# Two heads on each half of the PE rows, score products in pairs, sums inverted before they are spread, and keys rounded by GpSimd

## The reference

```python
qh = split(q @ Wq.T + bq)          # 16 heads of 8
kh = split(k @ Wk.T + bk)
vh = split(v @ Wv.T + bv)
scores = jnp.einsum('bhqd,bhkd->bhqk', qh, kh) / jnp.sqrt(jnp.float32(D_K))
scores = jnp.where(mask[:, None, None, :] == 0, jnp.float32(-1000000000.0), scores)
attn = jax.nn.softmax(scores, axis=-1)
out = jnp.einsum('bhqk,bhkd->bhqd', attn, vh)   # then @ Wo.T + bo
```

## Time and profile before

| | |
|---|---|
| median of 3 runs | 3891.91 us (3890.11 to 3892.72) |
| profiled execution | 3887.87 us |
| its span, first to last instruction | 3886.1 us |
| busy: PE, PEld, DVE, ACT, POOL | 86%, 63%, 65%, 53%, 30% of the span |
| mean granted TensorE clock | 0.935 |
| stage L1a, loop over batches | about 428 to 1235 us |
| stage L2a, loop over batches | about 1546 to 2336 us |

### The profile page before, as it was taken

One profiled execution on the slowest core, in us unless ns is written; L12 is line 12 of the kernel. 1 busy time (PEld: TensorE's weight loads), 2 busy tenths in 40 slices (PEclk: granted clock), 3 DMA queues, 4 the chain that ended last, 5 costly groups with the idle time before them and its releaser, 6 DMA issues. The chain is left out here.

```text
span 3886.1 us, 96641 instructions
## 1 busy us (share of the span) xinstructions
PE 3344.9 (86%) x40650; PEld 2451.9 (63%) x40650; DVE 2514.8 (65%) x3568; ACT 2066.9 (53%) x3842; POOL 1154.1 (30%) x1125
## 2 busy tenths in 40 slices
PE   6776799999998575999999996579999999999988
PEld 4455577777776563777777774346666666666654
DVE  5633577677774224777777773667878878778751
ACT  3211366566664111666566663367677776776733
POOL 0012312222121214222222111135455455554520
PEclk9877899999999686999999997689999999999989
DMA  7932666555561314555554530100000000000000
GB/s 226 254 120 72 176 165 167 157 150 157 162 167 31 106 38 116 129 132 133 124 124 123 129 92 7 22 24 17 25 25 17 24 18 23 25 17 25 17 1 26
DMA packets 137255, 345.88 MB, mean 89 GB/s; under 512 B 56179, under 2 KB 79547, under 8 KB 136827
## 3 DMA queue, kind: packets, MB, share of 16 engines
q1 hardware_dynamic: 134139, 334.22, 32.3%
q0 software_dynamic: 2688, 5.51, 0.5%
HBM read 174.63 MB, written 17.09 MB: 49 GB/s over the span
## 5 line engine op out<-in xcount | busy, mean ns | idle before, releaser
L2040 POOL TENSOR_TENSOR l_S<-l_S,l_shift 125x448 f32<-125x448 f32 (+1 forms) x416 | 461.1, 1147 | 329.0 <-ACT l_shift L2272 326.5
L1338 ACT ACTIVATE L1a_probs<-ps 125x448 f32<-125x448 f32 x768 | 383.2, 544 | 202.8 <-PE ps L1238 189.5
L1338 ACT ACTIVATE L2a_probs<-ps 125x448 f32<-125x448 f32 x768 | 382.9, 544 | 203.3 <-PE ps L1238 189.9
L1371 DVE TENSOR_REDUCE L2a_chunk_max<-ps 112x1 f32<-112x1000 f32 x256 | 300.9, 1196 | 147.4 <-PE ps L1197 147.0
L1371 DVE TENSOR_REDUCE L1a_chunk_max<-ps 112x1 f32<-112x1000 f32 x256 | 300.9, 1196 | 135.9 <-PE ps L1197 135.4
L2150 PE MATMUL ps<-l_S,l_z 125*128 125x448 f32 x768 | 344.3, 545 | 0.0
L2253 ACT ACTIVATE ctx_stats<-ps 125x512 f32<-125x512 f32 (+1 forms) x416 | 248.3, 597 | 180.0 <-PE ps L2098 170.8
L2317 DVE TENSOR_REDUCE l_norms<-ctx_stats 125x8 f32<-125x512 f32 (+1 forms) x416 | 268.1, 675 | 77.9 <-ACT ctx_stats L2253 77.8
L2343 DVE SCALAR_TENSOR_TENSOR l_S<-ps,l_neg_cols,l_inv_norms 125x448 f32<-125x448 f32 x384 | 256.1, 679 | 81.8 <-PE ps L2119 77.1
L1197 PE MATMUL ps<-L1a_keys,L1a_queries 98*112 98x500 f32 x768 | 264.6, 427 | 47.0 <-DVE L1a_chunk_max L1371 20.5
L1197 PE MATMUL ps<-L2a_keys,L2a_queries 96*112 96x500 f32 x768 | 264.6, 427 | 45.8 <-DVE L2a_chunk_max L1371 20.5
(11 more groups left out here) (478 smaller groups left out, 7071.3 us busy)
## 6 DMA issues: line engine op xcount, KB each, us to landing
L1a_keys<-L1a_k_hi SPq DMA_DIRECT2D x256, 187.5 KB
L2a_keys<-L2a_k_hi SPq DMA_DIRECT2D x256, 187.5 KB
a_ctx_T<-in_ctx_T SPq DMA_DIRECT2D x32, 750.0 KB, 11.7
L1a_ctx_T<-in_ctx_T SPq DMA_DIRECT2D x32, 750.0 KB, 6.1
xn<-L_valid SPq DMA_DIRECT2D x32, 750.0 KB, 7.6
L1a_keys<-L1a_k_lo SPq DMA_DIRECT2D x128, 187.5 KB
L2a_ctx_T<-in_ctx_T SPq DMA_DIRECT2D x32, 750.0 KB, 6.4
L2a_keys<-L2a_k_lo SPq DMA_DIRECT2D x128, 187.5 KB
```

The costliest lines, as they stand in the source:

```text
L1338: nc.scalar.activation(probs[t % NPR][:, h * HQ // 2:(h + 1) * HQ // 2], s.ps[0:KP, i % 3, 0:HQ // 2], ACT.Exp).then_inc(probs_made, 1)
L1371: ins = nc.vector.tensor_reduce(chunk_max[:, n, 0:1], product, AX.XY, ALU.max)
L2040: nc.gpsimd.tensor_tensor(S[b % 2][0:r, t, :], S[b % 2][0:r, t, :], shift[0:r, :], ALU.add)\
```

## The change

The array's rows are used as two halves of 64. A group g now has two heads (u = 0) on rows 0 to 63 and two (u = 1) on rows 64 to 127: 3 x 16 rows of parts, mask and maxima in each half, 50 or 52 rows. Products are made in pairs, one on each half, into different PSUM banks. For a tile the scores are eight products of 112 columns in place of four of 224; both halves are asked for at the start of a step, and the exponentials of the two halves follow. The 12 rows items are two products of 500 columns each, as before, of 48 to 50 rows. The key pieces have 16 rows: 24 DMAs a batch for 12. The maxima take 4 DMAs for 2, the query terms 6 for 3, the mask rows 2 for 1. All 128 rows of the keys are set to one at the start. `k_hi` is made by GpSimd in front of each subtraction. The sums are transposed to 112 x 8, inverted, widened to 32 columns each by VectorE ("sums"), and spread by two products two steps later ("spread"); the norm multiplies from PSUM.

```diff
-    G, HPG = 4, 4
-    GR, GC4 = HPG * DK, HPG * SQ
+    G = 4
+    HALF = D // 2
+    GR = 2 * DK
     KQ = 3 * GR
...
+    ROWS = G * NKC
+    PIECES = 2 * G * 3
...
     step_items[5].append(("sums", -1, 0))
+    step_items[7].append(("spread", -1, 0))
...
+                def move(u, g, k, part):
+                    first, row = (2 * g + u) * GR, u * HALF + k * GR
+                    sp.dma_start(keys[b % NKB][row:row + GR, g, :].bitcast(F32), part[first:first + GR, :].bitcast(F32))\
+                        .then_inc(keys_moved, 16)
...
                 sp.wait_ge(k_hi_made, b * 2 + 2)
                 for g in range(G):
-                    for k in (0, 2):
-                        sp.dma_start(keys[b % NKB][k * GR:(k + 1) * GR, g, :].bitcast(F32),
-                                     k_hi[g * GR:(g + 1) * GR, :].bitcast(F32)).then_inc(keys_moved, 16)
+                    for u in range(2):
+                        for k in (0, 2):
+                            move(u, g, k, k_hi)
                 sp.wait_ge(k_lo_made, b * 2 + 2)
                 for g in range(G):
-                    sp.dma_start(keys[b % NKB][GR:2 * GR, g, :].bitcast(F32),
-                                 k_lo[g * GR:(g + 1) * GR, :].bitcast(F32)).then_inc(keys_moved, 16)
+                    for u in range(2):
+                        move(u, g, 1, k_lo)
...
                 for k, part in enumerate((max_hi, max_lo)):
-                    sp.dma_start(queries[b % NQ][SHIFT + k:SHIFT + k + 1, :, :].bitcast(F32), part[:, b % 2, :].bitcast(F32))\
-                        .then_inc(row_moved, 16)
+                    for u in range(2):
+                        row = u * HALF + SHIFT + k
+                        sp.dma_start(queries[b % NQ][row:row + 1, :, :].bitcast(F32),
+                                     part[u * G:(u + 1) * G, b % 2, :].bitcast(F32)).then_inc(row_moved, 16)
...
-            def take_keys_lo(b, n):
+            def split_keys(b, n):
                 cols = key_cols(n)
+                pool.wait_ge(scratch_dve, by_dve[("keys", b, n)])
+                if b and n == 0:
+                    pool.wait_ge(keys_moved, b * 16 * PIECES)
+                nc.gpsimd.tensor_copy(k_hi[:, cols], k_full[:, cols]).then_inc(k_hi_made, 1)
                 pool.wait_ge(k_hi_made, b * 2 + n + 1)
...
-                for half, (r, k) in enumerate(halves_of_row(n)):
-                    mm = nc.tensor.matmul(s.ps[0:RW, bank(item) + half, 0:KC],
-                                          queries[b % NQ][0:SHIFT, r // 2, r % 2 * RW:(r % 2 + 1) * RW],
-                                          keys[b % NKB][0:SHIFT, r // 2, k * KC:(k + 1) * KC], start=True, stop=True)
+                g, k = n // NKC, n % NKC
+                for u in range(2):
+                    mm = nc.tensor.matmul(s.ps[0:RW, bank(item) + u, 0:KC], queries[b % NQ][half(u, SHIFT), g, :],
+                                          keys[b % NKB][half(u, SHIFT), g, k * KC:(k + 1) * KC], start=True, stop=True)
...
+            def scores(b, t):
+
+                i = (b * KT + t) * 2
+                if t == 0:
+                    pe.wait_ge(row_moved, b * 64 + 64)
                 if i < 3:
                     pe.wait_ge(q_made, NCH)
-                else:
-                    pe.wait_ge(probs_made, i - 2)
...
+                if i >= 2:
+                    pe.wait_ge(probs_made, i - 1)
+                for g in range(G):
+                    for u in range(2):
+                        mm = nc.tensor.matmul(s.ps[0:KP, (i + u) % 3, g * RW:(g + 1) * RW],
+                                              keys[b % NKB][half(u, KS), g, t * KP:(t + 1) * KP],
+                                              queries[b % NQ][half(u, KS), g, :],
+                                              start=True, stop=True, skip_group_check=True)
+                        if g == G - 1:
+                            mm.then_inc(scores_made, 1)
...
-                nc.scalar.activation(k_hi[:, cols], k_full[:, cols], ACT.Copy).then_inc(k_hi_made, 1)
...
+            def invert_sums(item):
+                kind, b, n = item
+                dve.wait_ge(products, made[item])
+                nc.vector.reciprocal(inv[:, :, :].rearrange("p w j -> p (w j)"), s.ps[0:RW, bank(item), 0:8])\
+                    .then_inc(inverted, 1)
```

More of the change, by code:

```diff
@@ L887, in attention_16_heads, with half @@
     NQ, NKB, NPR, GT = 3, 3, 6, 3
-    PAIRS, SINGLES = RT, RT // 2
-    ROWS = PAIRS + SINGLES
-    PIECES = 12
+    ROWS = G * NKC
+    PIECES = 2 * G * 3
+    def half(u, n):
+        return slice(u * HALF, u * HALF + n)
     before_scores = [("rows", 1, 0), ("rows", 1, 1)]
@@ L1206, in turn, with turn_sums, spread_inverses @@
                 nc.tensor.transpose(s.ps[0:RT, bank(item), 0:RW], max_col[:, :], s.ident[0:RW, 0:RW]).then_inc(products, 1)
-            def spread_sums(item):
+            def turn_sums(item):
                 kind, b, n = item
                 wait_for_banks(pe, item)
-                if b == 0:
-                    pe.wait_ge(prep, 3)
                 pe.wait_ge(acc_taken, b + 1)
-                nc.tensor.matmul(s.ps[:, bank(item), 0:4 * SQ], sum_rows[:, :, :].rearrange("p j i -> p (j i)"),
-                                 acc[:, :], start=True, stop=True).then_inc(products, 1)
+                for w in range(2):
+                    mm = nc.tensor.matmul(s.ps[0:RW, bank(item), w * 4:(w + 1) * 4], acc[:, w * RW:(w + 1) * RW],
+                                          s.ident[:, DK:D:32], start=True, stop=True, skip_group_check=True)
+                mm.then_inc(products, 1)
+            def spread_inverses(item):
+                kind, b, n = item
+                wait_for_banks(pe, item)
+                pe.wait_ge(scratch_dve, by_dve[("sums", b, 0)])
+                for w in range(2):
+                    mm = nc.tensor.matmul(s.ps[:, bank(item), w * RW:(w + 1) * RW], inv_wide[:, w, :, :].rearrange("p j i -> p (j i)"),
+                                          s.ident[0:RW, 0:RW], start=True, stop=True, skip_group_check=True)
+                mm.then_inc(products, 1)
             def make(item):
@@ L1225, in make @@
                     turn(item)
[L1226 to L1232 removed]
+                elif item[0] == "sums":
+                    turn_sums(item)
+                else:
+                    spread_inverses(item)
+            def scores(b, t):
+                i = (b * KT + t) * 2
+                if t == 0:
+                    pe.wait_ge(row_moved, b * 64 + 64)
                 if i < 3:
                     pe.wait_ge(q_made, NCH)
[L1235 to L1241 removed]
+                if i >= 2:
+                    pe.wait_ge(probs_made, i - 1)
+                for g in range(G):
+                    for u in range(2):
+                        mm = nc.tensor.matmul(s.ps[0:KP, (i + u) % 3, g * RW:(g + 1) * RW],
[4 more added lines that the diff above has]
+                            mm.then_inc(scores_made, 1)
             def values(b, t):
@@ L1253, in values @@
                     j, c = h % 4, h // 4
+                    at = (h // 2 % 2 * 2 * G + h // 4 * 2 + h % 2) * SQ
                     mm = nc.tensor.matmul(s.ps[32 * j:32 * j + DK + 1, 3, c * SQ:(c + 1) * SQ], v[b % 2][:, t, h, :],
-                                          probs[t % NPR][:, h * SQ:(h + 1) * SQ], start=(t == 0 and c == 0),
+                                          probs[t % NPR][:, at:at + SQ], start=(t == 0 and c == 0),
                                           stop=(t == KT - 1), skip_group_check=True)
@@ L1308, in take @@
             def take(item):
-                if item[0] == "keys":
-                    take_keys(item)
-                elif item[0] == "values":
+                if item[0] == "values":
                     take_values(item)
@@ L1369, in empty_rows @@
                 product = s.ps[0:RW, bank(item):bank(item) + 2, 0:KC]
[L1370 to L1375 removed]
+                nc.vector.tensor_reduce(chunk_max[:, :, n // NKC, n % NKC], product, AX.X, ALU.max).then_inc(scratch_dve, 1)
                 if n == ROWS - 1:
@@ L1436, in _ @@
             dve.wait_ge(cut, 2)
-            nc.vector.tensor_reduce(group_mask[:, :], head_mask[:, :].rearrange("p (g h) -> p h g", h=HPG), AX.X,
-                                    ALU.add).then_inc(prep, 1)
-            nc.vector.tensor_copy(sum_rows[:, :, :], bcast(s.ident[:, DK:D:32], 32, 2)).then_inc(prep, 1)
+            nc.vector.memset(group_mask[:, :], 1.0).then_inc(prep, 1)
+            dve.wait_ge(prep, 2)
+            for u in range(2):
+                nc.vector.tensor_reduce(group_mask[half(u, KQ), :],
+                                        head_mask[half(u, KQ), :].rearrange("p (m e) -> p e m", e=2), AX.X,
+                                        ALU.add).then_inc(prep, 1)
             for item in prologue:
```

137 lines of the change are left out of this document (63 added, 74 removed).

## The result

The changed kernel takes 4500.9 us (median of 4 runs, 4480.1 to 4512.8) against 3891.0 us (4 runs, 3884.2 to 3892.7) for the kernel before on the same chip: a ratio of 1.157, 95% interval 1.152 to 1.161, slower. The forecast was 4320 us, range 4000 to 4530: 429 us more than before, where it is 610. Its profiled execution took 4503.4 us, span 4501.7, mean granted clock 0.819 for 0.935.

A forecast was written before the change was run, and what follows sets the result against it. DMA issues delaying the context were to bound each batch: 380 us in the loops, 40 before them, 6 at the end, +426 on 3887.9 profiled, 4314, plus 4.0 for the median: say 4320 us, range 4000 to 4530.

The forecast's parts named there:

- The chain: Sync queue, turn to turn: 24 piece issues delay the context, keys' product waits; periods 31.4 (+6.1) and 32.3 us (+7.0).
- Rival D: Sync queue's waits come per issue, not per byte: pieces take 20.1 us, total 4480 us; chance 15%.
- A: Slower but TensorE-bound: pieces issued near the mask rows' pitch, context in time, period 26.6, some 4010 us; chance 15%.
- The TensorE terms: TensorE work per batch: gains and losses sum to +1.3 us, a period of 26.6 without the context wait.
- the score step: Score loop: whole-step scores wait for the previous exponential, 1.28 us for a step that took 0.9.
- -0.8 for the sums: Inverse of the sums: 1.55 us reciprocal ahead of two row items becomes two short operations, saving 0.8 us a batch.
- +1.42: Start of a batch: two more maxima issues before the first scores, costing 1.42 us.
- Halves side by side: Score loads: the two row halves load in pairs, eight loads taking 0.42 us per step, no gain.
- C: Loads of the two halves go one after another, scores 0.83 us a step, about 4345 us; chance 17%.
- The clock: Keys' product: some 4 us of TensorE idle before it lowers the granted clock, priced at 0.75 us a batch.
- GpSimd's copy: Making the keys' high parts: 1000-column copy taken as 1.2 us, bounds 0.38 and 2.33.
- the 40 forecast for what stands before the loops: Before the loops: extra pieces, terms and GpSimd work in one queue add 20 us a stage, 40 in all.

The follow-up runs named there:

- experiment 2: Kernel before the change, each key piece of 32 rows moved as two of 16 (24 DMAs a batch): 4211.7 us, ratio 1.082.
- 3: Kernel before the change, with 24 key pieces of 16 rows and the context issued behind the 16 high pieces: 4018.0 us, ratio 1.034.
- experiment 1: Changed kernel, context DMA of batch b+3 issued behind the 16 high key pieces, ahead of the 8 low ones: 4417.8 us, ratio 1.135.
- Experiment 6: Kernel before the change, both halves of a tile's scores asked for at once behind the previous step's exponential, rows item after: 3963.8 us, ratio 1.019.
- experiment 9: Kernel before the change, score products over rows 0 to 49 only, rest of each sum left out: 4140.4 us, ratio 1.062.
- Experiment 10: Kernel before the change, score products over 50 rows and rows products over 48, rest of each sum left out: 4197.4 us, ratio 1.076.
- 7: Kernel of experiment 1, each pair of rows products made twice into the same banks: 4352.2 us, ratio 1.121.
- experiment 4: Kernel before the change, only the sums turned to 112 x 8, inverted, widened and spread by two products: 3888.0 us, ratio 0.998.
- experiment 8: Kernel of experiment 1, scores half by half in the earlier order (u = 0, item, u = 1): 4310.3 us, ratio 1.108.

## Why the prediction was right, and where it was not

**The chain: right in the short batches.** In stage L2, forecast and median of the 27 batches after: first maxima issue 0.89, 0.88; first piece 4.0, 3.7; 24 pieces 17.3, 16.6 (0.69 apart; 0.71 in experiment 2); context issued 21.3, 20.4; landing 5.6, 5.8; landed 26.9, 26.0 us after the turn. The keys' product starts at 26.2 in the short batches, right behind the landing. In the long ones it starts at 30.4, and there the chain does not set the time: TensorE, at 0.50, comes later than the context by itself. So a piece of 16 rows is issued at nearly the price of one of 32, and the slack of 2.2 us is used up. Experiments 2 and 3 show this chain by itself, in the kernel before; in the changed one it is worth 1.9% (experiment 1). Rival D (0.836 apart) and A (0.46) are out by the pitch.

**The TensorE terms: right for the score step, and in sum partly by luck.** Forecast 1.28, measured 1.28 (2136.61 to 2137.89 above). Experiment 6 has 1.11: waiting for the exponential gives 0.2. The rest comes with the other parts of the change; I put it down to products in pairs, where both halves of a tile are done only at the end, which no run tests by itself. The two products of a rows item start 4 ns apart, as forecast. A TensorE-bound batch came to 26.9 (forecast 26.6; experiment 1), but two terms of that sum were off against each other: -0.8 for the sums was -0.13 (below), and the first scores come 1.07 us later than before (4.49 for 3.42) where I had +1.42.

**Halves side by side: right, C is out.** TensorE's load queue in the short batch, the answer to the earlier trace rows:

```profile
2136.61 0.51 PEld L1270 LDWEIGHTS ps<-L2a_queries,L2a_keys 50*125 50x125 f32 x8 [0.67 <-ACT L2a_probs L1363]
```

Eight loads span 0.51 for 0.29 of two before: with 0.19 for one, four slots 0.107 apart and not eight. The Trainium skill, "TensorEngine Tiling (Array Packing)" (Key Properties), says that tiles load and multiply independently, and that a change of mode drains the array: the 0.51 agrees with the first, the 0.18 of experiment 9 with the second.

**The clock: the step that failed.** I read from the earlier trace rows that a wait is followed by a stretch at 0.50, and priced it at 0.75 us behind the keys' product alone. In the short batches it was 2.3 there (product to turn 6.0 for 3.7), and this brings them to 32.3 for the forecast 31.4. What was missing are the long batches, 10 of 27 at 36.6: the forecast had the full clock everywhere else. The loops cost 255 us in stage L1 and 240 in L2 over 28 batches each, 9.1 and 8.6 a batch for 7.0 and 6.1. Experiment 10 shows the cause as far as it is known: with scores and rows items in half rows the clock falls though TensorE waits less than before (19 us in the 27 batches for 35). How much of the fall in the changed kernel is due to the rows, and how much to its waits, is not measured. That 4501 us lies inside the range is in part luck: its top was set for rival D, at 4480, and not for the clock. Experiment 1 shows what the clock did to the other argument: a kernel without the context's wait would not have been at rival A's 4010 but at 4418, since the two causes cover each other: the wait is worth 194 us with full rows (2 to 3) and 83 with half rows. The Trainium skill has a rule near this, "TensorE: Matmul & The Clock Gate" (A second HAM failure mode: psum-queue depth-cycling): short idles between groups of products make the clock swing. Experiment 6, with such idles and 1.00, and 10, with fewer than before and 0.83, don't bear it out as the cause here; 7, which filled some of them and gained a little clock, agrees with it for a small part.

**The small terms.** The sums were mis-sized: 0.13 us for 0.8, since TensorE had waited for the reciprocal 0.3 us a batch only (8.6 us in 27; gone in experiment 4) and the product that spreads the inverses is new. GpSimd's copy took 1.02 us, taken as 1.2 (between 0.38 and 2.33):

```profile
L1159 POOL CAST L2a_k_hi<-L2a_k_full 128x1000 fp32r<-128x1000 f32 x28 | 28.5, 1018 | 773.0 <-DVE L2a_k_full L1387 773.0
```

The first batch of each stage is 21 and 23 us longer (20 forecast), the last two periods 9 and 28 us together (6 forecast for both stages), and 39 us lie outside the periods. Of these 12 lie between the start of the two stages and their first turns and belong to the 40 forecast for what stands before the loops, so 56 for 40; for the rest I had nothing, 24 in the work of the last batches behind their turns and 3 ahead of both stages. 495 + 44 + 37 + 39 = 615 us, the difference of the spans.

## What to carry to other kernels

A transfer that is cut in two costs the queue two issues; ask what stands last in that queue, and by how much it is early. A TensorE bound that was read at one clock holds at that clock only: before products are made smaller in rows, look whether the profile has stretches of such products, and what clock was granted there. When two causes lie over each other, taking one away shows little; test each in the kernel that lacks the other.

## What the runs showed of the chip that was not expected

- With instructions and order unchanged, score and rows products over 48 to 50 rows for 96 to 100 brought the granted clock from 1.00 to 0.83 in stage L2 and 0.85 in L1, TensorE busy 97% (experiment 10). With the score products alone it was 0.94 and 0.98 (experiment 9).
- TensorE can be busy and stay at 0.50: the long batches spend 20 to 31 us there, and TensorE is busy 93% in the one shown (35.24 of 37.80 us).
- Loads of the two row halves do not keep the order of the program among them. In experiment 8 the four score loads of the first half stand ahead of both loads of a rows item, and the first of these starts after two of them:

```profile
2134.77 0.29 PEld L1269 LDWEIGHTS ps<-L2a_queries,L2a_keys 50*125 50x125 f32 x2 [0.82 <-DMA L2a_queries<-L2a_max_lo]
2134.93 0.17 PEld L1218 LDWEIGHTS ps<-L2a_keys,L2a_queries 48*112 48x112 f32 x1
2134.98 0.29 PEld L1269 LDWEIGHTS ps<-L2a_queries,L2a_keys 50*125 50x125 f32 x3
```

  A plain step takes 0.70 us there, for 0.90 before and 1.28 in the change, the shortest of the three; a whole batch at the full clock is not shorter (26.6 to 28.2 us in stage L1, for 25.3 before).
